# Gated feed-forward stage: where VectorE rounds the next group's rows

## What is computed

```python
def rmsnorm(x): return x * rsqrt(mean(x * x, -1) + 1e-6)
def activation_quant(x):
    scale = 127.0 / clip(max(abs(x), -1), 1e-5)
    return clip(round(x * scale), -128, 127) / scale
def bitlinear(x, w): return einsum('bsd,hd->bsh', activation_quant(rmsnorm(x)), weight_quant(w))
gate = silu(bitlinear(x, w_gate))            # 256 -> 1024
up = bitlinear(x, w_up)                      # 256 -> 1024
x = x + bitlinear(gate * up, w_down)         # 1024 -> 256, on layernorm(x)
```

## Time and profile before

| | |
|---|---|
| median of three runs | 1840.26 us (1838.95 to 1842.91) |
| profiled execution, its own time | 1840.84 us |
| its span in the profile | 1839.1 us |
| granted TensorE clock, mean over the span | 0.832 of full |
| busy share of the span | PE 72%, DVE 72%, ACT 60%, POOL 32% |
| first gate (L2953) to last sum (L2985) of this stage | 1476.1 to 1669.8 us |

### The profile page before, as it was taken

How to read it: one execution, slowest core, us unless ns; L and a number is a source line. 1 busy time by engine, 2 the same in 40 slices (tenths; PEclk the granted TensorE clock), 3 DMA queues, 4 the chain that set the end, 5 groups by cost and what they waited for, 6 DMA issues and landing times. The chain is left out here.

```text
span 1839.1 us, 32255 instructions
## 1 busy us (share of the span) xinstructions
PE 1329.7 (72%) x11572; PEld 842.1 (46%) x11572; DVE 1318.3 (72%) x2817; ACT 1103.6 (60%) x1564; POOL 580.3 (32%) x1046
## 2 busy tenths in 40 slices
PE   4999999999899759885266674699998266772111
PEld 2565666565777525554023333366665224341110
DVE  5788888887555246788699997366665578765996
ACT  4588888877222147776378887244443268784564
POOL 6556666643200231110134331111110011114663
PEclk9799999999999879997556767799999578776555
DMA  7567777765200023330100000211110400000211
GB/s 224 158 175 180 182 188 183 179 156 112 51 0 0 5 65 79 75 78 18 50 1 1 1 1 1 64 33 39 34 38 12 120 1 1 0 1 23 58 35 46
DMA packets 97396, 122.64 MB, mean 67 GB/s; under 512 B 30064, under 2 KB 82488, under 8 KB 92252
## 3 DMA queue, kind: packets, MB, share of 16 engines
q1 hardware_dynamic: 97244, 120.66, 25.5%
HBM read 82.17 MB, written 24.98 MB: 58 GB/s over the span
## 5 line engine op out<-in xcount | busy, mean ns | idle before, releaser
L1018 DVE TENSOR_REDUCE ratt_nmax<-ratt_psS 128x2 f32<-128x512 f32 x512 | 318.6, 683 | 62.5 <-PE ratt_psS L777 62.0
L914 ACT ACTIVATE ratt_E<-ratt_psT 128x1024 f32<-128x1024 f32 x256 | 255.1, 1022 | 74.2 <-PE ratt_psT L795 74.0
L777 PE MATMUL ratt_psS<-ratt_K,ratt_Q 72*128 72x256 bf16 x1024 | 203.1, 282 | 7.8 <-DVE ratt_nmax L1018 3.1
L795 PE MATMUL ratt_psT<-ratt_Q,ratt_K 75*128 75x256 bf16 x1024 | 196.8, 275 | 1.9 <-DMA ratt_Q<-ratt_rows 1.6
L819 PE MATMUL ratt_psO<-ratt_E,ratt_V 128*32 128x256 f32 x2048 | 138.8, 389 | 0.3 <-ACT ratt_E L914 0.3
L777 PEld LDWEIGHTS ratt_psS<-ratt_K,ratt_Q 72*128 72x128 bf16 x1024 | 80.6, 99 | 97.6 <-DVE ratt_nmax L1018 61.8
L795 PEld LDWEIGHTS ratt_psT<-ratt_Q,ratt_K 75*128 75x128 bf16 x1024 | 100.2, 99 | 19.6 <-issue 2.1
L3597 PE MATMUL final_psT<-final_identh,final_Z 128*128 128x128 f16 x64 | 8.2, 310 | 111.0 <-ACT final_Z L3631 111.0
L2389 PE MATMUL nffn_psH<-nffn_W,nffn_QT 128*128 128x512 bf16 x128 | 55.8, 586 | 31.5 <-ACT nffn_H L2468 20.3
L819 PEld LDWEIGHTS ratt_psO<-ratt_E,ratt_V 128*32 128x32 f32 x2048 | 53.8, 110 | 50.5 <-issue 27.7
L2589 POOL TENSOR_TENSOR all_X<-all_X,satt_bo 128x1024 f32<-128x1024 f32 x8 | 18.9, 2364 | 168.2 <-DVE all_X L2655 168.2
(11 more groups left out here) (468 smaller groups left out, 3702.1 us busy)
## 6 DMA issues: line engine op xcount, KB each, us to landing
ratt_K<-context_parts SPq DMA_DIRECT2D x96, 192.0 KB
ratt_Q<-z_parts SPq DMA_DIRECT2D x32, 576.0 KB
gatt_V<-in_ctx_dram SPq DMA_DIRECT2D x16, 512.0 KB, 6.6
context_parts<-ratt_CS SPq DMA_DIRECT2D x48, 128.0 KB, 6.5
z_parts<-ratt_ZS SPq DMA_DIRECT2D x48, 128.0 KB, 4.8
head_sums<-ratt_O SPq DMA_DIRECT2D x64, 72.0 KB
all_X<-in_x_dram SPq DMA_DIRECT2D x16, 256.0 KB, 4.0
ratt_C<-in_ctx_dram SPq DMA_DIRECT2D x16, 256.0 KB, 4.0
```

The costliest lines, as they stand in the source:

```text
L777: mm = nc.tensor.matmul(psS[:, RING[h], c * D:(c + 1) * D], Q9[0:R, buf, h, n % 2, c * P:(c + 1) * P], K9[0:R, buf, h, n % 2, :], start=Tr ...
L795: mm = nc.tensor.matmul(psT[:, j % 2, e, c, :], K9[0:RM, buf, h, u, c * P:(c + 1) * P], Q9[0:RM, buf, h, u, :], start=True, stop=True)
L914: sc.activation(E[:, m % 2 * 2 + p // 2, 2 * (p % 2):2 * (p % 2) + 2], psT[:, j % 2], ACT.Exp, scale=SCALE).then_inc(exped, 1)
L1018: v.tensor_reduce(nmax[:, n % 2, h, :], psS[:, RING[h]].rearrange("p (c t) -> p c t", c=2), AX.X, ALU.max, negate=True).then_inc(maxed, 1)
```

## The change

`round_up(g + 1)` moves up in VectorE's stream: from behind `gate(g, 3)` and `add(g - 1, 1)` to directly behind `z_scales(g + 1)`. No instruction is added or removed, and the streams of the other engines stay as they are.

```diff
                     if ahead:
                         z_maximum(g + 1)
                         z_scales(g + 1)
+                    if ahead:
+                        round_up(g + 1)
                     if a:
                         gate(g, 3)
                     if c:
                         add(g - 1, 1)
-                    if ahead:
-                        round_up(g + 1)
                     if a:
                         maximum(g, 3)
```

## The result

The changed kernel takes 1819.62 us (median of four runs, 1818.46 to 1823.36) beside 1839.85 us for the kernel before (four runs, 1838.95 to 1842.91): 20.2 us less, a ratio of 0.9898 with a 95% interval of 0.988 to 0.9915. The forecast was 1828.6 us in a range of 1821.5 to 1833.5. The sign and the path were right. The profiled execution took 1820.00 us, its span 1818.2.

What follows compares the result with a forecast made beforehand. No engine bounds the whole; each gated-stage turn is a VectorE stretch plus a round trip through TensorE and ScalarE. Clock cases of 10.1 and 13.3 us gave 11.7 us off the 1840.26 us median: 1828.6 us, range 1821.5 to 1833.5.

Steps and rivals of the forecast that it cites:

- What bounds the turn: Gated stage: 14.85 us of nearly gapless VectorE, then a round trip VectorE, TensorE, ScalarE, VectorE, mean 8.78 us.
- Step 1: VectorE's roundings skip gates and sum, 1.71 us, less 0.13 for a dependent start: net 1.58 us, 1.19 at g = 0.
- Step 2: TensorE's `turn_h` then waits for ScalarE's copy, leaving 1.49 of 1.58 us; round trip 7.62 us at the same clock.
- Every turn keeps its own clock, 10.1 us: Sum over the round trips with each turn's clock unchanged: 6 x 1.49 + 1.19 = 10.1 us gained.
- Step 3: Fourth gate 1.17 us later but 0.84 us before ScalarE's squares; ScalarE, delayed sums, GpSimd and SP queue cost zero.
- The slower rival: The fourth tile's later gate is on the path: 7 x 1.17 = 8.2 us slower, 1848.5 us, chance 0.05.
- Step 4: TensorE's idle ahead of `turn_z` shrinks from 3.54 to 1.96 us; round trip 7.62 at low clock, 5.96 at high.
- the middle between 10.1 and 13.3: Gain taken between turns keeping their clock and round trips halfway between low and high clock: 11.7 us.
- high clock throughout: Rival: all round trips at 2.4 GHz, ScalarE their limit; 18.5 us gained, 1821.8 us, chance 0.12.
- Against the clock part: Objection: TensorE's clock stayed at 0.50 through transposes, so earlier `turn_z` may not raise it; 8.2 us gained, 1832.1 us.
- the case in which transposes help the clock little: Rival: round trips stay at low clock, 8.2 us gained, 1832.1 us, chance 0.17.

Runs made afterwards that it cites:

- before_fill: The kernel before with 24 matmuls, results unread, in TensorE's idle stretch ahead of `turn_z`, roundings still late: 1827.02 us, ratio 0.9936.
- after_fill: The changed kernel with 12 matmuls, results unread, in TensorE's remaining idle stretch ahead of `turn_z`: 1819.05 us, ratio 0.9899.
- half_move: Against the kernel before, the roundings pass only the sum and stay behind the fourth gate, a shift of 0.39 us: ratio 0.9996.
- The larger sample: Both kernels run again without edits: changed 1819.37 us (six runs), before 1837.23 us (17 runs), ratio 0.9893.
- before_fill_turns: The kernel before with 48 transposes of 128x128, results unread, in TensorE's idle stretch ahead of `turn_z`: 1827.57 us, ratio 0.9942.

## Why the forecast was right and wrong

**What bounds the turn** was read rightly: VectorE's stretch is nearly constant (73.6 and 74.2 us in five turns) and the round trip is where the time comes from.

**Step 1**, the shift of 1.58 us with 0.20 us for the dependent start: the roundings start at 1549.29, 0.20 behind `zqs`. At equal high clock the whole shift is worth 1.57 us (before_fill against after_fill), at g = 0, at the low level, 1.18 us against 1.19 costed.

**Step 2**, the next wait at `turn_h`: it is there, but costs nothing at the high clock because ScalarE is the limit. Whether a turn that keeps its low clock would have gained the 1.49 us stays open. In the last turns of half_move a shift of 0.39 us was given back in the stretch; at g = 0 of the changed kernel 1.18 us were kept. "Every turn keeps its own clock, 10.1 us" was therefore not a safe floor.

**Step 3**, all zero: right. The delayed fourth gate ended at 1551.7, and ScalarE reached its squares at 1552.16, so 0.4 us of margin were left of the 0.84 costed. The slower rival had no ground.

**Step 4 and the sum over it** is what failed. The price of the high clock was right, 5.96 us forecast, 5.84 measured. Its frequency was not. The prediction held that 1.96 us of idle "speaks against a high clock as the rule"; this led to the middle between 10.1 and 13.3, which stands for a mean round trip of about 7.0 us, where 6.13 and 6.11 were measured, and "high clock throughout" got a chance of 0.12. The high clock held in four turns of six in both profiles, with TensorE idle for 1.96 to 2.19 us, and the others were at 6.41 to 6.84 us, about halfway. With 6 x (8.78 - 6.13) + 1.18 the round trips gave 17.1 us of the 18.5 allowed for the bound, and the stage as a whole 16.3, against 11.7 forecast.

**The range** lacked one thing more. Profiles differ by several microseconds ahead of the stage (1469.6 to 1476.1), and the three runs of the kernel before already span 4.0 us; I had added only 1.3 us, and that on the slow side alone. The gain of the stage alone, 16.3 us, would have put the time at 1824.0, within the range; the other 3.9 us of the 20.2 took it out. That they were chance is likely from the wander, and not proved: both profiles of the changed kernel begin the stage at 1471.6, both of the kernel before at 1475.0 or later. The larger sample does not settle it: the difference of its medians (17.9 us) would give 1822.4, inside the range, its ratio (0.9893) 1820.6, outside.

**Against the clock part**: the case in which transposes help the clock little had the low level of the earlier trace rows for it, with idle time right before it as the other reading. before_fill_turns filled that idle time with transposes and the clock stayed up, so the idle time is the cause.

## What to carry to other kernels

Where TensorE waits in every turn of a loop, price the wait twice: the time itself, and what the matmuls behind it cost at the low clock; here the clock alone was worth 11.1 us in the stage, and the shift on top of it 8.9, 20.0 together, of which the change without a filler got 16.3 to 17.0. A move that is too small to bring the clock back can be worth nothing, and a slightly larger one far more than its own length. Test it by filling the idle stretch with matmuls that nobody reads: it prices the clock alone, in one run. Compare such small changes by the stage in the trace, since the whole program wanders by more than they are worth.

## What the hardware showed that was not expected

- A step instead of a slope: a shift of the roundings by 0.39 us took nothing off the stage (ratio 0.9996), by 1.05 us it took 14.4 us off (ratio 0.9916). Low clock came into six round trips of six with a shift of 0 or 0.39 us, into two of six with 1.05, 1.32 and 1.58.
- In the turns g = 3 to 5 at the low clock the turn took 23.9 us whether the roundings came 0.39 us earlier or not: the stretch behind the round trip grew by what the round trip lost.
- 48 transposes kept the granted clock of the round trips at 1.00 as well as 24 matmuls of twice the columns did (round trips of 7.42 us with either).
